# Spreading the TensorE transposes of a step between its dense matmuls

## The chip, the cores and the metric

One NeuronCore of a Trainium2 chip runs the kernel. The metric is the time of one execution on the device, in microseconds (us). All times in this text that have a start are counted from the first instruction of the profiled execution.

## The reference

x has 64 sequences of 64 tokens with 512 features, in fp32. Four layers are added to it one after the other; the first, second and fourth take weights that an index of the sequence selects:

```python
x = x + (x @ W.T + (x @ A[idx0].T) @ Bm[idx0].T * scal[idx0])     # dense, and an adapter of rank 16
x = x + einsum('bct,bcd->bdt', x, w1[idx1])                       # mixes the 64 tokens of a sequence
x = x + attention(x, beta=min(cond, 4), Wq, Wk, Wv, Wo)           # 16 heads of 32, causal
x = x + einsum('bct,bcd->bdt', x, w3[idx3])
```

## The kernel before, in words

A pair is four sequences, 256 tokens, in two tiles (t = 0, 1) of 128 tokens; there are 16 pairs (PAIRS). Every engine has its own program, written out by hand, and the engines meet only at semaphores. A dense product of fp32 precision is made of three matmuls on operands split in a high and a low part (hi x hi, hi x lo, lo x hi). TensorE contracts over the partitions, so that x, x1 (after the second layer) and the probabilities must be transposed on TensorE: a transpose is a matmul of a 128 x 128 tile with the identity, and each matmul has a weight load of its own ahead of it.

The program is a software pipeline. Step i does attention, output product and last layer of pair i and, beside them, the first two layers and the keys of pair i + 1 (`if more`; the last of the 16 steps has no next pair). TensorE's order in a step (`step`, lines 532 to 574):

- `turn_x(i + 1)`, line 392: waits for x_in (loaded by SyncE) and for the copy of y, then eight transposes in banks 0 and 1. ScalarE (`x_hi`) and VectorE (`x_lo`) split the result into xT_hi and xT_lo.
- `queries(i)`, line 465: four blocks m of twelve matmuls of 256 columns. Then ScalarE and VectorE place them in q_bd (`place_queries`, `place_q`).
- `values(0)`, `scores(i, 0)`, `scores(i, 1)` (line 482), `values(1)`, `adapters_down(i + 1)`.
- The softmax goes meanwhile: VectorE scales, masks and takes the maximum, GpSimd subtracts it, ScalarE takes the exponential, VectorE sums and inverts. Tile 0 is multiplied by the inverse on GpSimd (line 958), tile 1 on VectorE (line 843), which give the semaphores probs_done[0] and probs_done[1].
- `layer0_dense(0)`: 12 matmuls of 512 columns (lines 415, 417, 419); `layer0_dense(1, ...)` for three of the four chunks: 9 more.
- `turn_probs(i, 0)`, line 487: waits for probs_done[0], then eight transposes (line 491); the 3 last products of `layer0_dense(1)`; `turn_probs(i, 1)`: waits for probs_done[1], then eight transposes. After each tile ScalarE and VectorE copy one half each to probsT.
- `attend(i, 0)` and `attend(i, 1)` (line 503), which wait for those copies.
- `adapters_up(i + 1)` (line 427), which waits for xa_parts. ScalarE makes xa_hi and xa_parts in `xa_hi_part` after its copy of the second tile to probsT, and attnT_hi after that.
- `layer2_out_hi(i, 0)` (line 514), `layer2_out_lo(i, 0)` (line 521), `layer1(i + 1)` (lines 435 to 438), half of `layer2_out_hi(i, 1)`: 4 matmuls, `turn_x1(i + 1)` (line 446): for each tile a wait for ScalarE's copy of x1 and four transposes, then the other 4 matmuls and `layer2_out_lo(i, 1)`. ScalarE and VectorE split the transposed x1 in `x1T_hi_part` and `x1T_lo_part`, for which the keys wait.
- `layer3(i, 0)`, half of `keys(i + 1)`, `layer3(i, 1)`, the other half of `keys`.

Of the kernel before, what the change touches and what calls it, by code (L numbers as in the profile page):

```python
# [31 lines left out]
P = 128  # L32
SEQS, S, D = 64, 64, 512
NC = D // P
TILES = 2
PT = TILES * P
# [4 lines left out]
HP = HEADS // 2  # L41
# [5 lines left out]
W0, WQ, WK, WV, WO = range(NW)  # L47
# [4 lines left out]
def cond_resid_kernel(nc, x, idx0, idx1, cond, idx3, W, A, Bm, scal, w1, Wq, Wk, Wv, Wo, w3, out):  # L52
# [7 lines left out]
    with ExitStack() as ctx:  # L60
# [9 lines left out]
        ident = sb("ident", [P, P])  # L70
# [13 lines left out]
        w_hi = sb("w_hi", [P, NW, NC, D], F32R)  # L84
        w_lo = sb("w_lo", [P, NW, NC, D], F32R)
# [5 lines left out]
        x_in = sb("x_in", [P, TILES, D])  # L91
# [156 lines left out]
        def tok(t):  # L248
            return slice(t * P, (t + 1) * P)
# [118 lines left out]
        def _(pe):  # L368
# [22 lines left out]

            def turn_x(i):
                pe.wait_ge(x_loaded, 16 * (i + 1))
                if not (isinstance(i, int) and i == 0):
                    pe.wait_ge(y_copied, 1 + TILES * (i - 1))
                for t in range(TILES):
                    for c in range(NC):
                        last = nc.tensor.transpose(bank[t][:, c * P:(c + 1) * P],  # L398
                                                   x_in[:, t, c * P:(c + 1) * P], ident[:])
                    last.then_inc(xT_mm, 1)  # L400

            def adapters_down(i):
# [8 lines left out]
                last.then_inc(xa_mm, 1)  # L411

            def layer0_dense(t, chunks=range(NC)):
                for c in chunks:
                    nc.tensor.matmul(bank[3 + t][:], xT_hi[:, c, tok(t)], w_hi[:, W0, c, :],  # L415
                                     start=(c == 0), stop=False)
                    nc.tensor.matmul(bank[3 + t][:], xT_hi[:, c, tok(t)], w_lo[:, W0, c, :],  # L417
                                     start=False, stop=False)
                    nc.tensor.matmul(bank[3 + t][:], xT_lo[:, c, tok(t)], w_hi[:, W0, c, :],  # L419
                                     start=False, stop=False)  # L420

# [8 lines left out]
            def layer1(i):  # L430

                pe.wait_ge(w1_ready, i + 1)
                for t in range(TILES):
# [5 lines left out]
                        .then_inc(x1_mm, 1)  # L439

            def turn_x1(i):

                for t in range(TILES):
                    pe.wait_ge(x1_copied, TILES * i + t + 1)
                    for c in range(NC):
                        last = nc.tensor.transpose(bank[(7 + t) % 8][:, c * P:(c + 1) * P],  # L446
                                                   x1[:, t, c * P:(c + 1) * P], ident[:])
                    last.then_inc(x1T_mm, 1)

            def project_T(w, first_bank, m):  # L450

                return split_products(
                    bank[first_bank + m // 2][:, (m % 2) * PT:(m % 2 + 1) * PT],
                    [(w_hi[:, w, c, m * P:(m + 1) * P], w_lo[:, w, c, m * P:(m + 1) * P],
                      x1T_hi[:, c, :], x1T_lo[:, c, :]) for c in range(NC)])

            def keys(i, chunks):
# [6 lines left out]

            def queries(i):
                pe.wait_ge(y_copied, 1 + TILES * i)
                for m in range(NC):
                    last = project_T(WQ, 2, m)
                last.then_inc(q_mm, 1)
# [16 lines left out]

            def turn_probs(i, t):
                pe.wait_ge(probs_done[t], i + 1)
                for hp in range(HP):
                    b = (5 + 2 * t + hp // 4) % 8  # L490
                    last = nc.tensor.transpose(bank[b][:, hp % 4 * P:(hp % 4 + 1) * P],  # L491
                                               probs[:, t, hp * P:(hp + 1) * P], ident[:])
                last.then_inc(pT_mm, 1)

# [12 lines left out]

            def layer2_out_hi(i, t, chunks=range(NC)):

                if chunks[0] == 0:  # L510
                    pe.wait_ge(attn_hi_done, TILES * i + t + 1)
                for c in chunks:
                    for m in (w_hi, w_lo):
                        nc.tensor.matmul(bank[5 + t][:], attnT_hi[:, c, tok(t)], m[:, WO, c, :],  # L514
                                         start=(c == 0 and m is w_hi), stop=False)

# [15 lines left out]
            def step(i, more=True):  # L532
                if more:
                    turn_x(i + 1)
                queries(i)
                if more:
# [8 lines left out]
                if more:  # L545
                    adapters_down(i + 1)
                    pe.wait_ge(v_placed, TILES * i + 1)
                    layer0_dense(0)
                    layer0_dense(1, range(NC - 1))
                turn_probs(i, 0)  # L550
                if more:
                    layer0_dense(1, [NC - 1])
                turn_probs(i, 1)
                attend(i, 0)
# [7 lines left out]
                if more:  # L562
                    layer1(i + 1)
                layer2_out_hi(i, 1, range(NC // 2))
                if more:
                    turn_x1(i + 1)
                layer2_out_hi(i, 1, range(NC // 2, NC))
                layer2_out_lo(i, 1)
# [458 lines left out]
```

## Time and profile before

| | us |
|---|---|
| median of 3 runs | 717.79 |
| lowest and highest | 717.52, 718.88 |
| span of the profiled execution | 715.9 |
| busy: TensorE | 688.1 (96%) |
| busy: VectorE | 420.5 (59%) |
| busy: ScalarE | 364.3 (51%) |
| busy: GpSimd | 156.3 (22%) |

One step takes 42.07 us and the steps are alike to a few hundredths. PE is TensorE with its matmuls, PEld are its weight loads, DVE is VectorE, ACT ScalarE and POOL GpSimd. In a row of the timeline the first number is the start and the second the time from the start of the first instruction to the end of the last one of the row; in brackets stands the idle time of the engine before it and what ended it. A matmul's row is longer than the time to the start of the next one, since matmuls overlap in the array: the start-to-start distance is what a matmul costs in a dense stretch.

### The profile page before, as it was taken

The numbers are of one execution on the slowest core, as the hardware profiler recorded it, in microseconds if no ns is written. First come the engines' busy times: TensorE is split into PE (matmuls) and PEld (weight loads), VectorE is DVE, ScalarE is ACT, GpSimd is POOL, SyncE is SP. The second block draws the span as 40 slices with busy tenths as digits, with TensorE's granted clock in tenths as the row PEclk, the third lists the DMA queues.
The fourth block names the chain that finished last, engine by engine and source line by source line (L and its number), as shares of the span: only waits on it lengthen the run. The fifth ranks groups of instructions, "written<-read, shape, count | busy, mean of one in ns | idle before, by whom it ended". The sixth has DMA issues, their size and how long they took to land.

```text
span 715.9 us, 14890 instructions
## 1 busy us (share of the span) xinstructions
PE 688.1 (96%) x5176; PEld 613.4 (86%) x5176; DVE 420.5 (59%) x627; ACT 364.3 (51%) x728; POOL 156.3 (22%) x146
## 2 busy tenths in 40 slices
PE   5799999999999999999999999999999999999986
PEld 4588898989889898998989889898988989898874
DVE  3656567375555647556564655647465674747463
ACT  3554555545454645455465545545544554554443
POOL 4104021130402204040220404013040401304030
PEclk9889999999999999999999999999999999999999
DMA  6520111102011110201111020110102011020000
GB/s 185 198 85 9 52 37 44 43 1 81 7 51 37 40 45 2 81 7 51 37 35 50 4 81 7 51 37 27 56 5 81 7 51 37 5 78 5 29 1 29
DMA packets 32767, 31.67 MB, mean 44 GB/s; under 512 B 18550, under 2 KB 18550, under 8 KB 32758
## 3 DMA queue, kind: packets, MB, share of 16 engines
q1 hardware_dynamic: 32758, 31.55, 14.0%
q8 instruction: 5, 0.08, 0.0%
q14 instruction: 4, 0.03, 0.0%
HBM read 22.61 MB, written 8.91 MB: 44 GB/s over the span
## 4 chain that ended last, share of the span: by engine, by line
PE 92%; SPq 3%; DMA 2%; DVE 2%; issue 1%; ACT 0%; POOL 0%; DVEq 0%
PE banks L387 13%; PE banks L388 13%; PE banks L389 13%; PE banks L514 9%; PE banks L482 8%; PE banks L503 5%; PE banks L521 4%; PE banks L415 4%; PE banks L417 4%; PE banks L419 4%; PE banks L491 4%; PE banks L446 2%; PE banks L408 2%; PE banks L398 2%; PE banks L427 2%; DMA b_parts<-b_lo 1%
## 5 line engine op out<-in xcount | busy, mean ns | idle before, releaser
L387 PE MATMUL banks<-x1T_hi,w_hi 128*128 128x256 f32 x512 | 146.0, 285 | 0.0
L389 PE MATMUL banks<-x1T_hi,w_lo 128*128 128x256 f32 x512 | 144.6, 283 | 0.0
L388 PE MATMUL banks<-x1T_lo,w_hi 128*128 128x256 f32 x512 | 144.6, 282 | 0.0
L936 POOL TENSOR_TENSOR w_bd<-w_in,ident 128x256 f32<-128x256 f32 x32 | 23.5, 734 | 477.3 <-PE banks L389 283.2
L388 PEld LDWEIGHTS banks<-x1T_lo,w_hi 128*128 128x128 f32 x512 | 97.8, 191 | 1.4
L387 PEld LDWEIGHTS banks<-x1T_hi,w_hi 128*128 128x128 f32 x512 | 97.8, 191 | 1.4
L389 PEld LDWEIGHTS banks<-x1T_hi,w_lo 128*128 128x128 f32 x512 | 97.8, 191 | 0.0
L759 DVE COPY k_bd<-banks 32x512 f32<-32x512 f32 x64 | 44.2, 691 | 79.1 <-PE banks L389 78.5
L958 POOL TENSOR_TENSOR probs<-probs,row_max 128x1024 f32<-128x1024 f32 x32 | 60.9, 1904 | 60.1 <-DVE row_max L834 60.1
L828 DVE SCALAR_TENSOR_TENSOR probs<-banks,beta,mask 128x512 f32<-128x512 f32 x64 | 46.4, 746 | 37.2 <-PE banks L482 36.6
L683 ACT ACTIVATE probs<-probs 128x1024 f32<-128x1024 f32 x32 | 33.9, 1060 | 65.2 <-POOL probs L958 64.8
L482 PEld LDWEIGHTS banks<-k_bd,q_bd 128*128 128x128 f32 x512 | 59.5, 192 | 2.9 <-issue 1.8
L838 DVE TENSOR_REDUCE row_sum<-probs 128x16 f32<-128x1024 f32 x32 | 39.0, 1220 | 38.6 <-ACT probs L683 38.6
L482 PE MATMUL banks<-k_bd,q_bd 128*128 128x128 f32 x512 | 59.8, 275 | 1.6 <-DVE q_bd L759 1.6
L606 ACT ACTIVATE v_bd<-banks 64x256 f32<-64x256 f32 x128 | 48.4, 378 | 24.8 <-PE banks L389 23.3
L606 ACT ACTIVATE k_bd<-banks 32x512 f32<-32x512 f32 x64 | 37.6, 587 | 39.5 <-PE banks L389 39.0
L514 PE MATMUL banks<-w_hi,attnT_hi 128*128 128x512 f32 x128 | 53.4, 417 | 0.0
L415 PE MATMUL banks<-w_hi,xT_hi 128*128 128x512 f32 x128 | 51.6, 403 | 0.0
L387 PE MATMUL banks<-w_hi,x1T_hi 128*128 128x512 f32 x128 | 51.4, 401 | 0.0
L514 PE MATMUL banks<-w_lo,attnT_hi 128*128 128x512 f32 x128 | 50.4, 393 | 0.0
L388 PE MATMUL banks<-w_lo,x1T_hi 128*128 128x512 f32 x128 | 50.1, 391 | 0.0
L417 PE MATMUL banks<-w_lo,xT_hi 128*128 128x512 f32 x128 | 50.0, 391 | 0.0
(110 smaller groups left out, 1388.7 us busy)
## 6 DMA issues: line engine op xcount, KB each, us to landing
x_in<-in_x_dram SPq DMA_DIRECT2D x16, 512.0 KB, 3.6
out_dram<-y SPq DMA_DIRECT2D x16, 512.0 KB, 2.8
b_sel<-b_parts SPq DMA_DIRECT2D x192, 32.0 KB, 1.8
w_in<-in_L_cond_weights_dram SPq DMA_DIRECT2D x128, 16.0 KB
probsT<-in_L_cond_W_dram SPq DMA_DIRECT2D x1, 1024.0 KB, 6.0
probs<-in_L_cond_Wk_dram SPq DMA_DIRECT2D x1, 1024.0 KB, 7.8
x_both<-in_L_cond_Wq_dram SPq DMA_DIRECT2D x1, 1024.0 KB, 10.0
probsT<-in_L_cond_Wv_dram SPq DMA_DIRECT2D x1, 1024.0 KB, 12.1
```

Of the source, the lines that this page charges most:

```text
L387: nc.tensor.matmul(out_ap, s_hi, m_hi, start=(k == 0), stop=False)
L388: nc.tensor.matmul(out_ap, s_hi, m_lo, start=False, stop=False)
L389: last = nc.tensor.matmul(out_ap, s_lo, m_hi, start=False, stop=(k == n - 1))
L415: nc.tensor.matmul(bank[3 + t][:], xT_hi[:, c, tok(t)], w_hi[:, W0, c, :], start=(c == 0), stop=False)
L417: nc.tensor.matmul(bank[3 + t][:], xT_hi[:, c, tok(t)], w_lo[:, W0, c, :], start=False, stop=False)
L482: last = nc.tensor.matmul(bank[b][:, hp % 4 * P:(hp % 4 + 1) * P], q_bd[:, t, hp, :], k_bd[:, t, hp, :], start=True, stop=True)
L514: nc.tensor.matmul(bank[5 + t][:], attnT_hi[:, c, tok(t)], m[:, WO, c, :], start=(c == 0 and m is w_hi), stop=False)
L606: return nc.scalar.activation(dst, src, ACT.Copy)
L759: return nc.vector.tensor_copy(dst, src)
L828: last = nc.vector.scalar_tensor_tensor(out=heads(probs[:, t, n * BANK:(n + 1) * BANK]), in0=heads(bank[(5 + 2 * t + n) % 8][:]), scalar=b ...
L838: nc.vector.tensor_reduce(row_sum[:, t, :], heads(probs[:, t, :]), AX.X, ALU.add).then_inc(sum_done, 1)
L958: nc.gpsimd.tensor_tensor(heads(probs[:, t, :]), heads(probs[:, t, :]), rows[:, t, :].unsqueeze(2).to_broadcast([P, HEADS, S]), op).then_i ...
```

## The change

The same instructions are issued in another order on TensorE. No other engine's program is touched.

- The eight transposes of x stand in the first two blocks of `queries`: tile t in block m = t, one transpose after the first of the three matmuls of each chunk (`project_T_and_turn_x`). Both of its waits stand ahead of the first block.
- Of the second half of layer 0 only chunk 0 (3 products) stands ahead of `turn_probs(i, 0)`. Six products are spread over its eight transposes and the three last ones over those of `turn_probs(i, 1)`: after transpose hp come the products hp * n // 8 to (hp + 1) * n // 8 - 1.
- The eight transposes of x1 stand one behind each of the eight matmuls of `layer2_out_hi(i, 1)`; the wait for tile 0 comes after the first of them, that for tile 1 after the fifth.

In the last step, and ahead of the loop, the order stays as it was.

```diff
+            def turn_x_ready(i):
                 pe.wait_ge(x_loaded, 16 * (i + 1))
                 if not (isinstance(i, int) and i == 0):
                     pe.wait_ge(y_copied, 1 + TILES * (i - 1))
+            def turn_x_chunk(t, c):
+                turned_chunk = nc.tensor.transpose(bank[t][:, c * P:(c + 1) * P],
+                                                   x_in[:, t, c * P:(c + 1) * P], ident[:])
+                if c == NC - 1:
+                    turned_chunk.then_inc(xT_mm, 1)
...
+            def layer0_product(t, c, n):
+                x_part, w_part = ((xT_hi, w_hi), (xT_hi, w_lo), (xT_lo, w_hi))[n]
+                nc.tensor.matmul(bank[3 + t][:], x_part[:, c, tok(t)], w_part[:, W0, c, :],
+                                 start=(c == 0 and n == 0), stop=False)
...
+            def turn_x1_chunk(i, t, c):
+                if c == 0:
+                    pe.wait_ge(x1_copied, TILES * i + t + 1)
+                turned_chunk = nc.tensor.transpose(bank[(7 + t) % 8][:, c * P:(c + 1) * P],
+                                                   x1[:, t, c * P:(c + 1) * P], ident[:])
+                if c == NC - 1:
+                    turned_chunk.then_inc(x1T_mm, 1)
...
+            def project_T_and_turn_x(w, first_bank, m, t):
+
+                out_ap = bank[first_bank + m // 2][:, (m % 2) * PT:(m % 2 + 1) * PT]
+                for c in range(NC):
+                    cols = slice(m * P, (m + 1) * P)
+                    nc.tensor.matmul(out_ap, w_hi[:, w, c, cols], x1T_hi[:, c, :], start=(c == 0), stop=False)
+                    turn_x_chunk(t, c)
+                    nc.tensor.matmul(out_ap, w_hi[:, w, c, cols], x1T_lo[:, c, :], start=False, stop=False)
+                    nc.tensor.matmul(out_ap, w_lo[:, w, c, cols], x1T_hi[:, c, :], start=False,
+                                     stop=(c == NC - 1))
...
-            def queries(i):
+            def queries(i, more):
                 pe.wait_ge(y_copied, 1 + TILES * i)
-                for m in range(NC):
+                if more:
+                    turn_x_ready(i + 1)
+                    for t in range(TILES):
+                        project_T_and_turn_x(WQ, 2, t, t)
+                else:
+                    for m in range(TILES):
+                        project_T(WQ, 2, m)
+                for m in range(TILES, NC):
                     last = project_T(WQ, 2, m)
                 last.then_inc(q_mm, 1)
...
+            def turn_probs(i, t, first, n):
+
                 pe.wait_ge(probs_done[t], i + 1)
                 for hp in range(HP):
-                    b = (5 + 2 * t + hp // 4) % 8
-                    last = nc.tensor.transpose(bank[b][:, hp % 4 * P:(hp % 4 + 1) * P],
-                                               probs[:, t, hp * P:(hp + 1) * P], ident[:])
-                last.then_inc(pT_mm, 1)
+                    turn_probs_chunk(t, hp)
+                    for k in range(first + hp * n // HP, first + (hp + 1) * n // HP):
+                        layer0_product(1, k // 3, k % 3)
...
+                pe.wait_ge(attn_hi_done, TILES * i + t + 1)
+                for c in range(NC):
+                    for n, m in enumerate((w_hi, w_lo)):
                         nc.tensor.matmul(bank[5 + t][:], attnT_hi[:, c, tok(t)], m[:, WO, c, :],
-                                         start=(c == 0 and m is w_hi), stop=False)
+                                         start=(c == 0 and n == 0), stop=False)
+                        if t == 1 and more:
+                            turn_x1_chunk(i + 1, c // 2, c % 2 * 2 + n)
...
-                if more:
-                    turn_x(i + 1)
-                queries(i)
+                queries(i, more)
...
                     layer0_dense(0)
-                    layer0_dense(1, range(NC - 1))
-                turn_probs(i, 0)
-                if more:
-                    layer0_dense(1, [NC - 1])
-                turn_probs(i, 1)
+                    layer0_dense(1, [0])
+                turn_probs(i, 0, 3, 6 if more else 0)
+                turn_probs(i, 1, 9, 3 if more else 0)
...
-                layer2_out_hi(i, 1, range(NC // 2))
-                if more:
-                    turn_x1(i + 1)
-                layer2_out_hi(i, 1, range(NC // 2, NC))
+                layer2_out_hi(i, 1, more)
```

## Rows read from the trace of the kernel before

**Rows 1.** The page: busy time of each engine, and the granted clock by slice.
```profile
PE 688.1 (96%) x5176; PEld 613.4 (86%) x5176; DVE 420.5 (59%) x627; ACT 364.3 (51%) x728; POOL 156.3 (22%) x146
...
PEclk9889999999999999999999999999999999999999
```

**Rows 2.** Waits from 100 to 670 us (total, times, longest); ScalarE's timeline at x_hi and place_queries.
```profile
PE banks L427 <- issue: 3.8, 14, 0.3
...
261.33 1.09 ACT L606 ACTIVATE xT_hi<-banks 128x512 fp32r<-128x512 f32 x2
...
265.55 1.19 ACT L606 ACTIVATE q_bd<-banks 64x512 f32<-64x512 f32 x2 [1.39 <-PE banks L389]
```

**Rows 3.** TensorE's matmuls in the timeline, around the transposes of x.
```profile
258.61 0.28 PE L389 MATMUL banks<-x1T_hi,w_lo 128*128 128x256 f32 x1
258.73 1.04 PE L398 MATMUL banks<-ident,x_in 128*128 128x128 f32 x8
...
259.72 0.28 PE L388 MATMUL banks<-x1T_lo,w_hi 128*128 128x256 f32 x1
```

**Rows 4.** TensorE's weight loads in the timeline, at two runs of transposes.
```profile
258.62 0.90 PEld L398 LDWEIGHTS banks<-ident,x_in 128*128 128x128 f32 x8
259.49 0.19 PEld L387 LDWEIGHTS banks<-x1T_hi,w_hi 128*128 128x128 f32 x1
...
279.92 1.03 PEld L491 LDWEIGHTS banks<-ident,probs 128*128 128x128 f32 x8
```

**Rows 5.** TensorE's matmuls in the timeline, from layer 0 to the adapters' product.
```profile
275.35 0.40 PE L415 MATMUL banks<-w_hi,xT_hi 128*128 128x512 f32 x1
...
280.15 1.04 PE L491 MATMUL banks<-ident,probs 128*128 128x128 f32 x8
280.94 0.47 PE L415 MATMUL banks<-w_hi,xT_hi 128*128 128x512 f32 x1
281.25 0.39 PE L417 MATMUL banks<-w_lo,xT_hi 128*128 128x512 f32 x1
...
281.71 1.03 PE L491 MATMUL banks<-ident,probs 128*128 128x128 f32 x8
282.68 2.13 PE L503 MATMUL banks<-probsT,v_bd 128*64 128x64 f32 x64
285.08 0.70 PE L427 MATMUL banks<-b_sel,xa_parts 96*128 96x512 f32 x2 [0.28 <-issue]
```

**Rows 6.** The last multiplications of the softmax in the timeline, tile 0 and 1.
```profile
276.78 1.90 POOL L958 TENSOR_TENSOR probs<-probs,row_inv 128x1024 f32<-128x1024 f32 x1
...
280.17 1.23 DVE L843 TENSOR_TENSOR probs<-probs,row_inv 128x1024 f32<-128x1024 f32 x1
```

**Rows 7.** Tile 0's multiplication and the loads behind it, in the last step.
```profile
695.75 1.90 POOL L958 TENSOR_TENSOR probs<-probs,row_inv 128x1024 f32<-128x1024 f32 x1
...
697.70 0.86 PEld L491 LDWEIGHTS banks<-ident,probs 128*128 128x128 f32 x8 [1.86 <-POOL probs L958]
```

**Rows 8.** ScalarE's timeline between the probabilities and the output product.
```profile
282.78 0.60 ACT L606 ACTIVATE probsT<-banks 128x512 f32<-128x512 f32 x1 [0.97 <-PE banks L491]
...
283.71 1.27 ACT L606 ACTIVATE xa_parts<-xa_hi 32x128 fp32r<-32x128 f32 x4
285.01 1.08 ACT L606 ACTIVATE attnT_hi<-banks 128x512 fp32r<-128x512 f32 x2
```

**Rows 9.** Timeline around the transposes of x1: copy of x1, output product, split, keys.
```profile
289.51 0.60 ACT L606 ACTIVATE x_both<-banks 128x512 f32<-128x512 f32 x1 [0.72 <-PE banks L438]
...
290.01 0.39 PE L514 MATMUL banks<-w_hi,attnT_hi 128*128 128x512 f32 x1
...
290.94 1.03 PE L446 MATMUL banks<-ident,x_both 128*128 128x128 f32 x8
...
292.81 0.68 DVE L763 TENSOR_TENSOR x1T_lo<-banks,x1T_hi 128x512 fp32r<-128x512 f32 x1
...
294.37 0.28 PE L387 MATMUL banks<-x1T_hi,w_hi 128*128 128x256 f32 x1
```

More of the change, by code:

```diff
@@ L390, in split_products @@
                 return last
-            def turn_x(i):
+            def turn_x_ready(i):
                 pe.wait_ge(x_loaded, 16 * (i + 1))
@@ L395, in turn_x @@
                     pe.wait_ge(y_copied, 1 + TILES * (i - 1))
+            def turn_x_chunk(t, c):
[3 more added lines that the diff above has]
+                    turned_chunk.then_inc(xT_mm, 1)
+            def turn_x(i):
+                turn_x_ready(i)
                 for t in range(TILES):
                     for c in range(NC):
-                        last = nc.tensor.transpose(bank[t][:, c * P:(c + 1) * P],
-                                                   x_in[:, t, c * P:(c + 1) * P], ident[:])
-                    last.then_inc(xT_mm, 1)
+                        turn_x_chunk(t, c)
             def adapters_down(i):
@@ L411, in adapters_down @@
                 last.then_inc(xa_mm, 1)
+            def layer0_product(t, c, n):
+                x_part, w_part = ((xT_hi, w_hi), (xT_hi, w_lo), (xT_lo, w_hi))[n]
+                nc.tensor.matmul(bank[3 + t][:], x_part[:, c, tok(t)], w_part[:, W0, c, :],
+                                 start=(c == 0 and n == 0), stop=False)
             def layer0_dense(t, chunks=range(NC)):
                 for c in chunks:
[L415 to L420, printed above, removed]
+                    for n in range(3):
+                        layer0_product(t, c, n)
             def adapters_up(i):
@@ L439, in layer1 @@
                         .then_inc(x1_mm, 1)
+            def turn_x1_chunk(i, t, c):
[5 more added lines that the diff above has]
+                    turned_chunk.then_inc(x1T_mm, 1)
             def turn_x1(i):
                 for t in range(TILES):
-                    pe.wait_ge(x1_copied, TILES * i + t + 1)
                     for c in range(NC):
-                        last = nc.tensor.transpose(bank[(7 + t) % 8][:, c * P:(c + 1) * P],
-                                                   x1[:, t, c * P:(c + 1) * P], ident[:])
-                    last.then_inc(x1T_mm, 1)
+                        turn_x1_chunk(i, t, c)
             def project_T(w, first_bank, m):
@@ L455, in project_T @@
                       x1T_hi[:, c, :], x1T_lo[:, c, :]) for c in range(NC)])
+            def project_T_and_turn_x(w, first_bank, m, t):
[3 more added lines that the diff above has]
+                    nc.tensor.matmul(out_ap, w_hi[:, w, c, cols], x1T_hi[:, c, :], start=(c == 0), stop=False)
+                    turn_x_chunk(t, c)
+                    nc.tensor.matmul(out_ap, w_hi[:, w, c, cols], x1T_lo[:, c, :], start=False, stop=False)
+                    nc.tensor.matmul(out_ap, w_lo[:, w, c, cols], x1T_hi[:, c, :], start=False,
+                                     stop=(c == NC - 1))
             def keys(i, chunks):
@@ L485, in scores, with turn_probs_chunk @@
                         last.then_inc(s_mm, 1)
-            def turn_probs(i, t):
+            def turn_probs_chunk(t, hp):
+                b = (5 + 2 * t + hp // 4) % 8
+                turned_chunk = nc.tensor.transpose(bank[b][:, hp % 4 * P:(hp % 4 + 1) * P],
+                                                   probs[:, t, hp * P:(hp + 1) * P], ident[:])
+                if hp == HP - 1:
+                    turned_chunk.then_inc(pT_mm, 1)
+            def turn_probs(i, t, first, n):
                 pe.wait_ge(probs_done[t], i + 1)
                 for hp in range(HP):
-                    b = (5 + 2 * t + hp // 4) % 8
-                    last = nc.tensor.transpose(bank[b][:, hp % 4 * P:(hp % 4 + 1) * P],
-                                               probs[:, t, hp * P:(hp + 1) * P], ident[:])
-                last.then_inc(pT_mm, 1)
+                    turn_probs_chunk(t, hp)
+                    for k in range(first + hp * n // HP, first + (hp + 1) * n // HP):
+                        layer0_product(1, k // 3, k % 3)
             def attend(i, t):
@@ L506, in attend, with layer2_out_hi @@
                 last.then_inc(av_mm, 1)
[L508 to L513, printed above, removed]
+            def layer2_out_hi(i, t, more=False):
+                pe.wait_ge(attn_hi_done, TILES * i + t + 1)
+                for c in range(NC):
+                    for n, m in enumerate((w_hi, w_lo)):
                         nc.tensor.matmul(bank[5 + t][:], attnT_hi[:, c, tok(t)], m[:, WO, c, :],
-                                         start=(c == 0 and m is w_hi), stop=False)
+                                         start=(c == 0 and n == 0), stop=False)
+                        if t == 1 and more:
+                            turn_x1_chunk(i + 1, c // 2, c % 2 * 2 + n)
             def layer2_out_lo(i, t):
```

## The prediction

> **What bounds the kernel now.** I read the share of each engine first. TensorE is busy for 96% of the span and nobody else for more than 59%, with the clock at full speed in all slices but the first few [rows 1]. Then I asked which waits TensorE has once the loop runs: between 100 and 670 us there is one kind only, 0.3 us ahead of line 427, once in each step [rows 2]. So everything outside that spot is work of TensorE back to back. A gain must make that work shorter, and a loss must put a wait into it. Starts are what counts, since the records of neighbouring matmuls overlap.
>
> I then took the pitch (start to start) of the kinds that the change mixes. A dense matmul of 256 columns is followed by the next after 0.12 us [rows 3]. One of 512 columns takes (280.15 - 275.35) / 21 = 0.2286 us: 21 of them stand between those two starts [rows 5]. A run of eight transposes starts at 258.73, and the second dense matmul after it at 259.72. Less the first dense one, 0.12, the eight took 0.87, or 0.109 each [rows 3]. The row of the first dense matmul after a run begins too early and is longer by as much (280.94, 0.47 where its kind takes 0.39, and the next only at 281.25), so it waited with its weights not yet there [rows 5].
>
> **Part 1, the mixing itself: no gain.** The step has 32 transposes, 8 of x, 16 of the probabilities, 8 of x1, and none is removed. The question is whether a transpose that has dense neighbours costs less than 0.109. The weight loads answer it. The load of the first transpose starts at 258.62, with the last dense matmul (258.61). The eight loads take 0.90, the last of them 0.14, so their starts are (0.90 - 0.14) / 7 = 0.109 apart. The dense matmul's load starts at 259.49, when the eighth transpose starts. At the 512-column neighbour, too, the load comes only 0.23 us ahead of its transpose, at the dense matmul's start [rows 4]. So a load never starts before the start of the matmul ahead of it, however long that one is, and from the start of a transpose to that of its follower 0.109 passes, whether the follower is a transpose or dense. A lone transpose between dense matmuls meets these same two borders: dense to transpose, 0.12 or 0.23 as before, and transpose to dense, 0.109. All 32 keep their price, and mixing gives nothing.
>
> The Trainium skill has a rule that speaks otherwise: its page "TensorE: Matmul & The Clock Gate" (Engine queue depths) says that TensorE's queue of 64 can pull weight loads ahead of matmuls in flight. The trace shows such a pull only by one place. The same page (LDWEIGHTS) gives columns / 1.2 GHz, which is an estimate of 107 ns for 128 columns, and the 109 ns agrees. If the first rule hid the load of a dense matmul behind a lone transpose, it would be the first rival below; by the second alone the sum stays as it is.
>
> Each new border from a transpose to a dense matmul could cost something. 8 x 0.109 + 0.12 = 0.99 is what rows 3 show for a run and its border, so it is nothing to the hundredth. There are 21 new borders outside the old ones (7 in the queries, 7 in the output product, 7 in the probabilities), bounded by 0 and 0.01 each. I take 0.04 us a step, nearer to the row, and 0 to 0.2 for the range.
>
> **Part 2, the probabilities: the wait comes earlier.** Before, nine products of the second half of layer 0 stood ahead of the wait for probs_done[0]; now three do. The first transpose could start at 280.15 - 6 x 0.2286 = 278.78 [rows 5]. GpSimd ends the multiplication that it needs at 276.78 + 1.90 = 278.68 [rows 6]. What a released wait costs is seen in the last step, where TensorE stood idle. GpSimd ended at 695.75 + 1.90 = 697.65 and the load started at 697.70, 0.05 later. The eight loads took 0.86 there, and with six pitches of 0.109 and a last load of 0.14 this leaves 0.06 from the first load to its transpose [rows 7]. So here the start is 278.68 + 0.05 + 0.06 = 278.79: just in time, the cover of 1.4 us is used up.
>
> The second wait isn't in time. Eight transposes and six products end at 278.79 + 0.872 + 1.372 = 281.03. VectorE ends its multiplication at 280.17 + 1.23 = 281.40 [rows 6], so the transpose starts at 281.40 + 0.11 = 281.51, after about 0.48 us of idle time. Nothing that ends at 281.40 is moved: it hangs on the scores, and turn_x plus queries have the same length together as before. Before, that transpose started at 281.71 and its three products were already done. Now two of the three lie ahead of the eighth transpose, so this one starts at 281.51 + 7 x 0.109 + 2 x 0.2286 = 282.73, against 281.71 + 0.763 = 282.47. That is 0.26 later. attend starts after the third product at 281.51 + 0.872 + 0.686 + 0.10 = 283.17. The 0.10 is what stands between the run's end and attend in before. This is 0.49 later than 282.68 [rows 5].
>
> Who waits for that: ScalarE copies the second half of the probabilities at 282.78, then makes xa_hi and xa_parts, until 283.71 + 1.27 = 284.98, and then attnT_hi. It has no gap in this chain, and line 427 on TensorE starts only at 285.08, after its 0.28 us of idle time [rows 5, 8]. The label of that gap is "issue", but 284.98 is what fits. With the eighth transpose 0.26 later ScalarE's chain is 0.26 later, and line 427 starts at 285.34. attend, 2.13 long, ends at 283.17 + 2.13 = 285.30, which is inside that. So of the 0.49 lost ahead of attend, 0.23 is paid by the old gap, and 0.26 us a step is left. After it TensorE is the bound, and nothing gives it back.
>
> **Part 3, the transposes of x in queries.** The same 8 transposes and 48 matmuls; queries end when they did. The signal for the first tile comes 10 x 0.12 = 1.2 us later and that for the second 22 x 0.12 = 2.6 us later. Behind them ScalarE has x_hi, select_a and keep_x1, then place_queries, before which it was idle for 1.39 us [rows 2]. It started x_hi only at 261.33, busy with the keys until then, and was through with both tiles at 261.33 + 1.09 = 262.42 [rows 2]. The second tile is now turned at 258.73 + 22 x 0.12 + 8 x 0.109 = 262.24, and with the end of the record, about 0.2 later, ScalarE starts it at 262.45, and not at 261.88: 0.6 late, less than the 1.39. I cost this at nothing; without that cover it would be up to 0.6 a step. The waits for x_in and y stand where they stood, at the head of the step.
>
> **Part 4, the transposes of x1 in the output product.** Two waits move. The first stood after four dense matmuls and now stands after one. ScalarE's first copy of x1 ends at 289.51 + 0.60 = 290.11, and the load may start at 290.16, where it could have started at 290.01 and its transpose at 290.24 [rows 9]. The transpose starts at 290.16 + 0.06 to 0.11: 0 to 0.03 late, I take 0.03 for it with the second wait. The second, after five dense and four transposes, is needed at 291.4 and is long there. The eighth transpose moves from 290.94 + 0.763 = 291.70 to 290.01 + 8 x 0.2286 + 7 x 0.109 = 292.60, its record ends 0.27 later, and with ScalarE's 0.60 and VectorE's 0.68 behind it x1T_lo ends at about 294.25 (292.81 + 0.68 = 293.49 before). keys start at 294.37 and their load one matmul earlier, at about 294.14 [rows 9]. With the release, 294.30, this is 0 to 0.1 late; the start 0.06 after the load makes it about nothing. VectorE's add for the second tile waits behind it for 0.3 us; layer3's second tile is 2.9 us away.
>
> **The sum.** 0.26 + 0.04 + 0.03 = 0.33 us a step, in 15 steps (the last has no next pair and keeps its order): 5.0 us. The profiled execution took 715.9, so 720.9; the median of the runs is 717.8, 1.9 above it, so 722.8.
>
> **Rivals.** (a) Faster: a load slips under a lone transpose. If TensorE holds the weights of a dense matmul ready two places ahead, a transpose with a dense follower costs 0.06 (what a first transpose needs after its load [rows 7]) and not 0.109. That saves 16 x 0.05 = 0.8 a step in queries and in the output product, and 0.10 of the 0.26: 0.33 - 0.9 = -0.57, or 709.2. It decides from 0.088 a transpose downwards. Against it stand all the loads of rows 4; for it, that no row shows a transpose with a dense neighbour on both sides. Chance 0.13. (b) No change: lone transposes get a little cheaper, about 0.09, and that pays for the wait; or the multiplications come earlier in the new order. 717.8, chance 0.10. (c) Slower still: line 427 and what follows take over the whole 0.49 of attend, because attend is slower to start after a dense matmul than after a transpose, or ScalarE's chain is held by the later attend. 15 x (0.49 + 0.07) = 8.4, 726.2, chance 0.15; with the upper bounds of the borders and of part 4 the main case reaches 717.8 + 15 x (0.26 + 0.2 + 0.1) = 726.2 too. (d) The waits are as forecast: 722.8, chance 0.62.
>
> **Range and chances.** The main case runs from 721.7 (0.26 alone) to 726.2. The range goes down to the case without change, and leaves out (a): 717.5 to 726.5. A measurement of this kernel can tell 0.2%, 1.4 us. Faster by more 0.14, within 0.10, slower by more 0.76.
>
> **What would show it.** Right: TensorE's waits list the probability transposes with VectorE's multiplication as releaser, 0.4 to 0.5 us in each of 15 steps; the gap ahead of the adapters' product shrinks from 0.28 to below 0.1; the pitch after a lone transpose is 0.109, and a query block of 12 dense and 4 transposes takes 1.87 us. Wrong: that block takes 1.7 or less (a), or the wait is listed for less than 0.2 us a step (b), or idle time stays ahead of the adapters' product besides the new wait (c).

## The result and the profile after

The changed kernel takes 723.08 us (median of 4 runs, 722.25 to 723.50) and the kernel before 718.25 (4 runs): a ratio of 1.0066, with a 95% interval of 1.0054 to 1.0078. It is slower by 4.8 us. Forecast were 722.8 and 5.0 us.

The profiled execution of the changed kernel has a span of 721.6 us. Its busy row and clock, to be held beside rows 1:

```profile
span 721.6 us, 14905 instructions
PE 694.4 (96%) x5176; PEld 605.6 (84%) x5176; DVE 422.9 (59%) x627; ACT 373.0 (52%) x728; POOL 156.6 (22%) x146
PEclk9789999999999999999999999999999999999998
```

TensorE's instructions are the same 5176, and from 72 us on the granted clock is 1.00 in both. The busy share hasn't moved either, and says nothing on this change. The step tells more. From the start of the adapters' product (line 427, now 435) in the first step to that in the fifteenth, the kernel before takes 663.76 - 74.73 = 589.03, or 42.07 a step, and the changed one 669.50 - 75.75 = 593.75, or 42.41: 0.34 a step, 5.1 us in 15 steps. The other 0.6 us between the two profiled spans lies ahead of the first of these marks, in a part that differs by some tenths and up to 2 us between the profiled runs of this study. The granted clock was lower there in the profile of the changed kernel: 0.79 from 18 to 36 us and 0.83 from 36 to 54 us, against 0.83 and 0.88.

TensorE's wait for VectorE's multiplication of tile 1 over the whole execution (total, times, longest), first in the changed kernel, then in the kernel before:

```profile
PE banks L520 <- DVE probs L875: 4.1, 16, 0.8
```
```profile
PE banks L491 <- DVE probs L843: 0.8, 1, 0.8
```

TensorE waits for it in each of the 16 steps now, and did so in the last one alone before. The 0.3 us ahead of the adapters' product [rows 2] is gone. Both stand in TensorE's timeline of one step (start, length, line; in brackets the idle time before and its releaser), which answers to rows 5:

```profile
281.22 0.40 PE L520 MATMUL banks<-ident,probs 128*128 128x128 f32 x2
281.37 0.48 PE L422 MATMUL banks<-w_hi,xT_hi 128*128 128x512 f32 x1
281.69 0.27 PE L520 MATMUL banks<-ident,probs 128*128 128x128 f32 x1
...
283.89 0.55 PE L520 MATMUL banks<-ident,probs 128*128 128x128 f32 x3 [0.22 <-DVE probs L875]
284.19 0.48 PE L422 MATMUL banks<-w_hi,xT_hi 128*128 128x512 f32 x1
...
285.62 2.13 PE L541 MATMUL banks<-probsT,v_bd 128*64 128x64 f32 x64
287.79 0.70 PE L435 MATMUL banks<-b_sel,xa_parts 96*128 96x512 f32 x2
```

This step's scores start at 270.53, those of the step in rows 5 at 268.10, so 2.43 is to be taken off to set the two side by side. Tile 1's transposes start behind an idle time, attend (line 541) starts 0.51 later than before (285.62 - 2.43 = 283.19 against 282.68), and the adapters' product (line 435) 0.28 later (285.36 against 285.08), now with no gap ahead of it. The mean over 13 steps, counted from the start of the scores, is the same: 0.52 for attend and 0.28 for the adapters' product.

Rows 3 and 4 have their answer in the block of queries with lone transposes. First the matmuls, then the weight loads:

```profile
261.17 0.28 PE L475 MATMUL banks<-x1T_hi,w_hi 128*128 128x256 f32 x1
261.30 0.27 PE L398 MATMUL banks<-ident,x_in 128*128 128x128 f32 x1
261.32 0.36 PE L477 MATMUL banks<-x1T_lo,w_hi 128*128 128x256 f32 x1
261.52 0.28 PE L478 MATMUL banks<-x1T_hi,w_lo 128*128 128x256 f32 x1
261.64 0.28 PE L475 MATMUL banks<-x1T_hi,w_hi 128*128 128x256 f32 x1
...
263.04 0.28 PE L475 MATMUL banks<-x1T_hi,w_hi 128*128 128x256 f32 x1
```
```profile
261.19 0.14 PEld L398 LDWEIGHTS banks<-ident,x_in 128*128 128x128 f32 x1
261.30 0.19 PEld L477 LDWEIGHTS banks<-x1T_lo,w_hi 128*128 128x128 f32 x1
261.41 0.19 PEld L478 LDWEIGHTS banks<-x1T_hi,w_lo 128*128 128x128 f32 x1
```

One transpose and three dense matmuls take 261.64 - 261.17 = 0.47, and 3 x 0.12 + 0.109 is 0.47. The whole block, 12 dense matmuls and 4 transposes, takes 263.04 - 261.17 = 1.87, as forecast. The load of the dense matmul behind the transpose starts at 261.30, with the transpose, and the next load at 261.41. So the dense matmul got going at 261.41, 0.11 behind the transpose; its row begins at 261.32 and is 0.36 long where its neighbours have 0.28, for it waited for its weights.

### The profile page after: what moved, and what is told of

It reads as the page before. It is cut to its first block, busy times and chain, and to the rows that moved or that the text cites. A ratio compares the mean times of both kernels' runs of the same rounds, so it can differ in the third digit from the quotient of the medians.

```text
span 721.6 us, 14905 instructions
## 1 busy us (share of the span) xinstructions
PE 694.4 (96%) x5176; PEld 605.6 (84%) x5176; DVE 422.9 (59%) x627; ACT 373.0 (52%) x728; POOL 156.6 (22%) x146
## 4 chain that ended last, share of the span: by engine, by line
PE 81%; DVE 7%; ACT 6%; DMA 2%; issue 2%; SPq 1%; POOL 0%; DVEq 0%
PE banks L387 11%; PE banks L389 11%; PE banks L388 11%; PE banks L551 9%; PE banks L513 8%; PE banks L541 5%; PE banks L560 4%; ACT v_bd L638 3%; DVE probs L875 3%; DVE row_sum L870 3%; PE banks L520 2%; ACT probs L715 2%; PE banks L452 2%; PE banks L415 2%; PE banks L478 2%; PE banks L475 2%
## 5 line engine op out<-in xcount | busy, mean ns | idle before, releaser
L387 PE MATMUL banks<-x1T_hi,w_hi 128*128 128x256 f32 x392 | 111.7, 285 | 0.0
L388 PE MATMUL banks<-x1T_lo,w_hi 128*128 128x256 f32 x392 | 110.8, 283 | 0.0
L389 PE MATMUL banks<-x1T_hi,w_lo 128*128 128x256 f32 x392 | 110.7, 283 | 0.0
L387 PEld LDWEIGHTS banks<-x1T_hi,w_hi 128*128 128x128 f32 x392 | 74.8, 191 | 4.1 <-DVE x1T_lo L795 3.4
L388 PEld LDWEIGHTS banks<-x1T_lo,w_hi 128*128 128x128 f32 x392 | 74.9, 191 | 0.7
L389 PEld LDWEIGHTS banks<-x1T_hi,w_lo 128*128 128x128 f32 x392 | 74.9, 191 | 0.0
L520 PE MATMUL banks<-ident,probs 128*128 128x128 f32 x256 | 51.2, 276 | 5.5 <-DVE probs L875 4.1
L551 PE MATMUL banks<-w_lo,attnT_hi 128*128 128x512 f32 x128 | 55.5, 433 | 0.0
L422 PE MATMUL banks<-w_lo,xT_hi 128*128 128x512 f32 x128 | 54.1, 422 | 0.0
L422 PE MATMUL banks<-w_hi,xT_lo 128*128 128x512 f32 x128 | 53.9, 421 | 0.0
```

Of the source, the lines that this page charges most:

```text
L387: nc.tensor.matmul(out_ap, s_hi, m_hi, start=(k == 0), stop=False)
L388: nc.tensor.matmul(out_ap, s_hi, m_lo, start=False, stop=False)
L389: last = nc.tensor.matmul(out_ap, s_lo, m_hi, start=False, stop=(k == n - 1))
L422: nc.tensor.matmul(bank[3 + t][:], x_part[:, c, tok(t)], w_part[:, W0, c, :], start=(c == 0 and n == 0), stop=False)
L520: turned_chunk = nc.tensor.transpose(bank[b][:, hp % 4 * P:(hp % 4 + 1) * P], probs[:, t, hp * P:(hp + 1) * P], ident[:])
```

## The experiments

Two theories stood at the start. The first is that of the prediction: a transpose costs 0.109 us wherever it stands, and the loss comes from waits that stand earlier in TensorE's order, above all that for tile 1 of the probabilities. The rival: each border between a transpose and a dense matmul costs something. The change has 21 more of them, and 5 us / 15 / 21 would be 0.016 each.

Steps are measured as above, from the adapters' product of the first step to that of the fifteenth, over 14, each from one profiled execution; the kernel before has one profile, against which all steps are held. Medians of one group belong beside the kernel before of the same group.

| kernel | step, us | against before | ratio (95% interval) |
|---|---|---|---|
| before | 42.07 | | |
| changed | 42.41 | +0.34 | 1.0066 (1.0054 to 1.0078) |
| x only | 42.09 | +0.02 | 1.0000 (0.9988 to 1.0013) |
| probabilities only | 42.33 | +0.26 | 1.0066 (1.0043 to 1.0089) |
| x1 only | 42.16 | +0.08 | 1.0016 (1.0004 to 1.0028) |
| nine and none | 42.13 | +0.06 | 1.0016 (1.0003 to 1.0030) |
| six and six | 43.04 | +0.97 | 1.0210 (1.0181 to 1.0239) |
| before, xa early | 41.64 | -0.43 | 0.9904 (0.9871 to 0.9938) |
| changed, xa early | 42.37 | +0.29 | 1.0064 (1.0041 to 1.0088) |
| before, xa on ScalarE | 41.56 | -0.51 | 0.9876 (0.9854 to 0.9899) |
| changed, xa on ScalarE | 42.14 | +0.07 | 1.0007 (0.9995 to 1.0019) |

### Each part alone

From the changed kernel, the other two parts put back. x only:

```diff
-                    layer0_dense(1, [0])
-                turn_probs(i, 0, 3, 6 if more else 0)
-                turn_probs(i, 1, 9, 3 if more else 0)
+                    layer0_dense(1, [0, 1, 2])
+                turn_probs(i, 0, 9, 0)
+                if more:
+                    layer0_dense(1, [3])
+                turn_probs(i, 1, 12, 0)
...
-                        if t == 1 and more:
-                            turn_x1_chunk(i + 1, c // 2, c % 2 * 2 + n)
```
(with `turn_x1(i + 1)` after half of the output product again)

> Only the eight transposes of x are spread (over the first two blocks of queries); the probabilities and x1 keep the order of before. Theory (a lone transpose costs 0.109 us like one in a run, and the loss of the change comes from waits that stand earlier): a step of 42.07 us and 718.3 us, no change. Rival (each border between a transpose and a dense matmul costs something, and that is where the 5 us went): 7 of 21 new borders, a third of 5 us, so a step of 42.18 and 720.0. Second rival (lone transposes are cheaper, and a wait elsewhere hid it): a step below 42.0.

Measured: 718.35 against 717.95, and a step of 42.09. The rival wants 0.11 more a step for its seven new borders, and the step is 0.015 longer. Even that doesn't lie at the borders. In the mean of 13 steps, the stretch from the first matmul of the keys to the end of the queries, which holds all eight transposes, is 0.015 shorter than before (13.038 against 13.053), and the twelve matmuls of values(1), of which nothing was moved, take 0.03 longer (2.849 against 2.817). Why they take longer is open. So a border to a matmul of 256 columns costs nothing that this run shows, and no transpose got cheaper. The part is worth nothing either way, as forecast. But its cover was thinner than I had reckoned, see below.

Probabilities only, with `turn_x(i + 1)` ahead of the queries again, as well as the run of x1:

```diff
-                    turn_x_ready(i + 1)
-                    for t in range(TILES):
-                        project_T_and_turn_x(WQ, 2, t, t)
+                    turn_x(i + 1)
+                    for m in range(TILES):
+                        project_T(WQ, 2, m)
```

> Only the products of layer 0 and the transposes of the probabilities are mixed, 6 products in the first tile and 3 in the second. Theory: TensorE waits about 0.48 us for VectorE's multiplication, 0.23 of it is paid by the old gap ahead of the adapters' product, 0.26 a step is left: a step of 42.34 and 718.3 + 15 x 0.26 = 722.2. Rival (borders): a step of 42.18, 720.0.

Measured: 722.56 against 717.95, and a step of 42.33, 0.26 longer. Its waits between 100 and 670 us, matmuls and then weight loads (total, times, longest):

```profile
PE banks L520 <- DVE probs L875: 2.9, 14, 0.2
```
```profile
PEld banks L520 <- DVE probs L875: 7.3, 14, 0.5
```

This part alone makes three quarters of the loss, and its wait is the one on VectorE. The row of the weight loads is the better measure. The dense matmul ahead of the wait has a record of 0.48 where its pitch is 0.23, so that idle time counted from the record's end comes out too small: 0.2 for a delay of 0.5.

x1 only: the products of layer 0 put back as in x only, and `turn_x(i + 1)` ahead of the queries as in probabilities only.

> Only the transposes of x1 are spread over the output product of tile 1. Theory: the first transpose waits 0.02 to 0.03 for ScalarE's copy, and the keys' first load waits about 0.05 for VectorE's x1T_lo: a step of 42.15, 718.3 + 15 x 0.075 = 719.4. Rival (borders): 42.18, 720.0, with no wait of the keys' load.

Measured: 719.23 against 717.95, and a step of 42.16, 0.08 longer. The waits of the weight loads, in the same stretch:

```profile
PEld banks L387 <- DVE x1T_lo L797: 2.9, 13, 0.2
PEld banks L452 <- ACT x_both L640: 2.5, 13, 0.2
```

Both forecast waits are there: the keys' first load for VectorE's x1T_lo, and the first transpose for ScalarE's copy of x1. These 0.075 were forecast after the changed kernel had been measured; the prediction itself had 0.03 and its borders for this part. The three parts add up to 0.36, the whole has 0.34.

### Mixing with no late wait, and with a later one

Nine products among the transposes of tile 0, none among those of tile 1, x and x1 as before:

```diff
-                turn_probs(i, 0, 3, 6 if more else 0)
-                turn_probs(i, 1, 9, 3 if more else 0)
+                turn_probs(i, 0, 3, 9 if more else 0)
+                turn_probs(i, 1, 12, 0)
```

> All nine movable products of layer 0 are mixed with the transposes of the first tile of the probabilities and none with those of the second; x and x1 as before. The first wait is as early as in the change, the second stands after all twelve products, as in before. Theory (the second wait alone makes the loss): both tiles on time, no idle time of TensorE at either, a step of 42.07 and 718.3. Rival (mixing layer 0 with the transposes costs by itself, or the first wait does): a step of 42.2 or more, over 720.

Measured: 718.93 against 717.95, and a step of 42.13. No wait on either tile is left in the list of the matmuls, and of the 0.26 nothing but 0.06 remains. So the place of the second wait makes the loss, and mixing doesn't. The 0.06 had not been forecast here. Its timeline at tile 0 (eight borders to a dense matmul of 512 columns, three of them shown), and a row of the weight loads' waits between 100 and 670 us:

```profile
321.91 0.29 PE L520 MATMUL banks<-ident,probs 128*128 128x128 f32 x1
...
322.28 0.27 PE L520 MATMUL banks<-ident,probs 128*128 128x128 f32 x1
322.30 0.48 PE L422 MATMUL banks<-w_lo,xT_hi 128*128 128x512 f32 x1
322.62 0.27 PE L520 MATMUL banks<-ident,probs 128*128 128x128 f32 x1
...
324.00 0.27 PE L520 MATMUL banks<-ident,probs 128*128 128x128 f32 x1
324.03 0.48 PE L422 MATMUL banks<-w_hi,xT_hi 128*128 128x512 f32 x1
324.35 0.27 PE L520 MATMUL banks<-ident,probs 128*128 128x128 f32 x1
```
```profile
PEld banks L520 <- POOL probs L990: 3.1, 14, 0.2
```

Five pairs of a transpose and a dense matmul take 324.00 - 322.28 = 1.72, 0.344 each, where 0.109 + 0.2286 is 0.338. So such a pair costs 0.006 more than its two parts; on which of its two borders that falls, the rows don't show. The seven new pairs make 0.04 of the 0.06. The other 0.02 is at the first transpose: its load waits for GpSimd, and its pair takes 322.28 - 321.91 = 0.37, 0.03 more than the others. The rival was right in kind, and its size is little more than a third of what it would need.

None of the second half of layer 0 ahead of the wait, six products in each tile:

```diff
-                    layer0_dense(1, [0])
-                turn_probs(i, 0, 3, 6 if more else 0)
-                turn_probs(i, 1, 9, 3 if more else 0)
+                turn_probs(i, 0, 0, 6 if more else 0)
+                turn_probs(i, 1, 6, 6 if more else 0)
```

> The dose of the second wait: no product of the second half of layer 0 stands ahead of the probabilities, six are mixed with the first tile and six with the second; x and x1 as before. Theory (what the late copy of the second tile costs is set by ScalarE's chain behind its eighth transpose): the transposes of the second tile again start at VectorE's multiplication, the eighth has five products ahead of it in place of none, so it is 0.26 + 3 x 0.2286 = 0.95 us later than in before. A step of 43.02, 718.3 + 15 x 0.95 = 732.5. Rival (TensorE's own delay counts in full): 0.49 + 3 x 0.2286 = 1.17 a step, 43.24 and 735.9.

Measured: 733.25 against 718.74, and a step of 43.04, 0.97 longer. The theory forecast 0.95 and its rival 1.17. The waits of the weight loads, in the same stretch:

```profile
PEld banks L520 <- POOL probs L989: 11.7, 13, 0.9
PEld banks L520 <- DVE probs L874: 6.8, 13, 0.5
PEld banks L553 <- ACT attnT_hi L637: 4.0, 13, 0.3
```

The wait that grew is the first one, for GpSimd and tile 0 (0.2 in the changed kernel). The second, for VectorE and tile 1, is 0.5 as it was. What was dosed is the number of products behind the second wait, and with it the time of the eighth transpose. Against before, attend starts 1.21 later and the adapters' product 0.97 later (means of 13 steps from the start of the scores), so again 0.24 of TensorE's own delay doesn't count. The load of the output product behind it waits 0.3 for attnT_hi, as before the change, and ScalarE starts attnT_hi right behind xa_parts (290.61, after 289.32 + 1.27 = 290.59). That is the chain from the eighth transpose of tile 1 over ScalarE's copy, xa_hi and xa_parts. But attend ends at 288.52 + 2.13 = 290.65, within 0.1 us of it, so that this run alone doesn't tell whether the chain or the end of attend sets the adapters' product.

### What the old gap paid

VectorE sums xa and scales it between the two sums of the softmax; ScalarE makes xa_hi and xa_parts ahead of its copies of the probabilities. TensorE's program isn't touched. First on the kernel before:

```diff
                 sums(i, 0)
+                if more:
+                    sum_xa(i + 1)
+                    scale_xa(i + 1)
                 sums(i, 1)
...
                     if more and t == 0:
-                        sum_xa(i + 1)
-                        scale_xa(i + 1)
-                if more:
-                    xa_lo_part(i + 1)
+                        xa_lo_part(i + 1)
...
+                if more:
+                    xa_hi_part(i + 1)
                 for t in range(TILES):
                     act.wait_ge(pT_mm, TILES * i + t + 1)
                     copy(probsT[:, t, 0:BANK], bank[(5 + 2 * t) % 8][:]).then_inc(pT_copied_act, 1)
-                if more:
-                    xa_hi_part(i + 1)
```

> The kernel before with another order on ScalarE and VectorE: xa_sum and xa are made on VectorE between the two sums of the softmax (it was idle 1.9 us there), xa_hi and its copies on ScalarE ahead of the copies of the probabilities (idle 2.6 us there). TensorE's order is that of before. Theory (the 0.28 us ahead of the adapters' product is ScalarE's chain xa_hi, xa_parts, and the next matmul waits for attnT_hi behind it): the gap goes, 0.28 to 0.4 us a step, a step of about 41.7 and 713 us. Rival (the gap is TensorE's own, a wait against a register or the change of tile shape): 42.07, 718.3.

Measured: 712.87 against 718.74, and a step of 41.64. The gap that the profile labels "issue" [rows 2, 5] was ScalarE's chain: with the chain out of the way it is gone, and so is the wait for attnT_hi behind it, 0.43 a step together. The edit moves VectorE's part of this work too. Before, it ended at 284.29, 0.7 ahead of ScalarE's 284.98, so it wasn't what the product waited for:

```profile
283.71 0.58 DVE L763 TENSOR_TENSOR xa_parts<-xa,xa_hi 32x128 fp32r<-32x128 f32 x2 [0.23 <-ACT xa_hi L606]
```

The label says only that the profile found no releaser.

The same on the changed kernel:

> The changed kernel with the same new order on ScalarE and VectorE as in the kernel with xa made early. Theory: now nothing pays back a part of the 0.49 us that attend starts late, so the step is 0.49 + 0.07 longer than that of the kernel before with xa made early: about 42.25, and 5 + 15 x 0.23 = 8.4 us above it, so about 721.5. Rival (the old gap paid nothing): the distance stays 5.0 us.

Measured: 722.19 against 718.74, and a step of 42.37, which is 0.72 above its partner and not 0.56. VectorE's and GpSimd's timelines (of the kernel before with xa early; in the changed one the rows have the same lengths) show what had been added:

```profile
317.34 1.84 DVE L783 TENSOR_TENSOR xa<-xa_sum,scal_rows 64x256 f32<-64x256 f32 x1
319.11 1.20 DVE L838 TENSOR_REDUCE row_sum<-probs 128x16 f32<-128x1024 f32 x1
```
```profile
317.00 1.91 POOL L958 TENSOR_TENSOR probs<-probs,row_inv 128x1024 f32<-128x1024 f32 x1
```

The scaling takes 1.84 us where it took 0.42. It starts beside GpSimd's multiplication and ends at 319.18, 0.27 after that one's end (318.91). The second sum, and everything up to tile 1's wait, is 0.25 late. The Trainium skill has this in "SBUF — State Buffer" (SBUF: two separate sides): a VectorE instruction with two SBUF inputs and a GpSimd instruction that reads SBUF take turns for a whole instruction, and the one that comes second stands still. By that rule the scaling would run after 318.91. It ended 0.27 after it where it takes 0.42 alone, so the trace agrees to within 0.15 us; no run here shows the port itself.

So the two kernels were run again with the scaling on ScalarE, ahead of xa_hi, as four activations of 64 columns with a scale per partition (and VectorE's `xa_lo_part` waiting for them). The edit is against the kernels with xa early, and `scale_xa` is gone from VectorE:

```diff
+            def scale_xa(i):
+                act.wait_ge(xa_summed, i + 1)
+                for n in range(PSEQ):
+                    last = nc.scalar.activation(xa[:, n * S:(n + 1) * S], xa_sum[:, n * S:(n + 1) * S], ACT.Copy,
+                                                scale=scal_rows[:, bass.ds(i, 1), n:n + 1].rearrange("p a b -> p (a b)"))
+                last.then_inc(xa_scaled, 1)
...
                 if more:
+                    scale_xa(i + 1)
                     xa_hi_part(i + 1)
```

> As the kernel before with xa made early, but the scaling of xa stands on ScalarE, ahead of xa_hi, in place of VectorE. On VectorE it took 1.84 us beside GpSimd's multiplication (0.42 where GpSimd is idle) and made the second sum and all behind it 0.25 late. Theory: VectorE's second sum starts at once behind the exponential again, the second tile's transposes are on time, and the step goes from 41.65 to about 41.60: 712 to 713 us. Rival (the second sum was late for another reason): VectorE's second multiplication is as late as with xa made early, and the step stays at 41.65.

Measured: 710.49 against 719.32, and a step of 41.56. VectorE's and ScalarE's timelines:

```profile
314.58 0.35 DVE L786 TENSOR_TENSOR xa_sum<-banks,xa_low 64x256 f32<-64x256 f32 x1
316.59 1.22 DVE L847 TENSOR_REDUCE row_sum<-probs 128x16 f32<-128x1024 f32 x1 [1.67 <-ACT probs L690]
```
```profile
315.50 1.06 ACT L690 ACTIVATE probs<-probs 128x1024 f32<-128x1024 f32 x1
316.47 1.05 ACT L632 ACTIVATE xa<-xa_sum,scal_rows 64x64 f32<-64x64 f32 x4
```

The second sum starts 0.03 behind the exponential's end (316.56), as in before. The 0.08 gained over xa early is more than the 0.05 forecast, and the median lies below the 712 to 713. The sum of xa, which has one input in PSUM, takes 0.35 here; it starts 0.16 ahead of the same multiplication (314.74), runs beside it for 0.19, and that one is 1.91 long as ever. This is the fastest kernel of the study, 1.2% below before.

> The changed kernel with the same two edits. Theory (the 0.28 us ahead of the adapters' product paid 0.23 of the 0.49 that attend starts late): without that gap the step is 0.49 + 0.08 longer than with the old order of TensorE and the same two edits, so about 42.16 and 8.5 us above it. The missed number of the changed kernel with xa made early (0.72 and not 0.56 above its partner) came from VectorE's 0.25, which counted in full there. Rival (the gap paid nothing): the distance is 0.34 a step, 5 us. Second rival (another 0.16 is lost in the changed order when xa is early): 0.72, 10.8 us.

Measured: 719.58 against 719.32, and a step of 42.14, 0.58 above its partner (forecast 0.57). So the old gap did pay. Against its partner, attend starts 0.52 later, as in the changed kernel against before, and the adapters' product 0.52 later too, where it was 0.28 with the gap (means of 13 steps from the start of the scores). The same change of order costs 0.34 a step in a kernel with the gap, and 0.58 in one without. The difference of 0.24 is the 0.23 of the prediction.

## Why the prediction was right

All forecast places are in the frame of rows 5; those measured are less 2.43.

| | forecast | measured |
|---|---|---|
| first transpose, tile 0 | 278.79 | 278.79 |
| first transpose, tile 1 | 281.51 | 281.46 (its load) + 0.06 |
| attend | 283.17 | 283.19 |
| adapters' product | 285.34 | 285.36 |
| step longer by | 0.33 | 0.34 |
| median, us | 722.8 | 723.08 |

- **Part 1, the pitch of a lone transpose.** Right. The load never starts ahead of the matmul before its own, with dense neighbours on both sides too, and rival (a) fell with the load rows of the changed kernel. The 0.04 for borders was of the right size, but I had put it evenly: those to a 256-column matmul cost nothing that a run shows, and a pair with a 512-column matmul costs 0.006. The probabilities have eight new borders and not seven (nine against one); five of these lie ahead of the second wait and count for nothing.
- **Part 2, the wait for tile 1.** Right in place and size: 0.26 forecast and 0.26 measured where it stood alone. That the old gap pays 0.23 of 0.49 is what the last pair shows. It had been an inference from "284.98 fits".
- **Part 3, the transposes of x.** Right in the sum, too optimistic in its cover. I let ScalarE lose 0.6 us of the 1.39. Its timeline in the changed kernel:

```profile
263.79 0.60 ACT L638 ACTIVATE xT_hi<-banks 128x512 fp32r<-128x512 f32 x1
264.87 0.60 ACT L638 ACTIVATE xT_hi<-banks 128x512 fp32r<-128x512 f32 x1 [0.48 <-PE banks L398]
265.60 0.31 ACT L638 ACTIVATE a_sel<-a_all 128x128 fp32r x1
266.32 0.31 ACT L638 ACTIVATE a_sel<-a_all 128x128 fp32r x1 [0.41 <-issue]
...
267.97 1.04 ACT L638 ACTIVATE x_both<-x_both 128x1024 f32<-128x1024 f32 x1
268.92 1.18 ACT L638 ACTIVATE q_bd<-banks 64x512 f32<-64x512 f32 x2
```

  Before, the four activations of select_a stood behind a backlog and ran in 0.91 us. Now ScalarE has caught up, and each of the last three has 0.40 of "issue" ahead of it: 2.46 us in all. It is so in all four kernels that spread the transposes of x (changed, x only, and the changed ones with xa early and with xa on ScalarE), and in none of the seven others. In the code each needs a register that ScalarE loads itself; that this load is what takes the 0.40 is inferred, no run tests it. place_queries starts at 268.92, at 266.49 in the frame of before, against 265.55 [rows 2]: 0.94 late. It ends at 270.10. The scores start at 270.53 and their first weight load at 270.31, so 0.2 us of cover is left. It cost nothing, but the step that I missed is that an engine that catches up with its work can show issue times that a backlog had hidden. The 1.39 of idle time was used up, and more. That values(0) stands between the queries and the scores was a second cover, which I had not counted; that the part costs nothing is by this cover, and in so far luck.
- **Part 4, the transposes of x1.** The waits are the right ones, the size isn't: 0.03 for them and a third of the 0.04 for borders were forecast, and 0.08 measured alone, of which 7 x 0.006 = 0.04 are borders. The first transpose loses 0.01 or less. The keys' wait, which I had put at about nothing, is about 0.05. The weight loads of the changed kernel show the step that was wrong:

```profile
297.04 0.19 PEld L387 LDWEIGHTS banks<-x1T_hi,w_hi 128*128 128x128 f32 x1 [0.22 <-DVE x1T_lo L795]
297.15 0.19 PEld L388 LDWEIGHTS banks<-x1T_lo,w_hi 128*128 128x128 f32 x1
```

  The next load comes with the start of the matmul, so the keys' first matmul started 0.11 after its load, where I had taken 0.06. Part 4 came out 0.04 above its forecast and the whole 0.02 below the sum of its parts; that 0.33 stands so near to 0.34 is partly luck.
- **The signs that I named.** The gap ahead of the adapters' product is gone and the block takes 1.87, as named. One sign was badly chosen. I expected TensorE's waits to list 0.4 to 0.5 us a step and took less than 0.2 as a sign for rival (b). The list of the matmuls gives 0.22, for the reason told above; the row of the loads, 0.5, is what I should have named.
- **The rivals.** (b), no change, falls with the probabilities alone. (c), the whole 0.49, is what happens once the gap is gone, and only then.

## What to carry to other kernels

Where weight loads go only one place ahead, as here, a short matmul costs its follower's load time wherever it stands, and spreading short matmuls among long ones buys nothing; measure a load's start against the matmul before its own to see it. What such a change does is to move waits: for each one, set its new place beside the end of the work it waits for, and follow the consumers of what comes late up to the first idle time that pays for it. An idle time with no releaser in the profile is worth an experiment of its own, since here it was another engine's chain, and taking that chain out of the way gave 1.2%, more than the whole change of TensorE's order cost.

## What the runs showed of the hardware

- A transpose and a dense matmul of 512 columns behind it take 0.344 us as a pair, 0.006 more than apart; next to matmuls of 256 columns nothing is lost that a run shows.
- A weight load starts with the start of the matmul before its own and not earlier, also between short and long ones (261.30 and 261.41 in the changed kernel).
- VectorE's scaling with two SBUF inputs took 1.84 us and not 0.42 when it started beside GpSimd's multiplication; its sum with an input in PSUM took 0.35 with 0.19 of it beside that.
- ScalarE's activations of select_a, whose address comes from a register that it loads itself, have 0.40 us of "issue" between them when ScalarE isn't behind with its work (2.46 us for four), and none when it is (0.91).
